# The passage from the adjacency product to the recurrence: the last layer norm in halves on two engines, the recurrence's first step beside it, and VectorE's weight preparation in the last block

## The reference

```python
x = x + relu(adj @ (item_feat @ W_item.T + b_item) + layernorm(x) @ W_user.T + b_user)
u = layernorm(x)
# LSTM over all 10000 tokens, hidden size 128, gates i, f, g, o of W_ih u + W_hh h + b
# g = argmax of two logits of h (0 or 1); w = g * h; inc = cumsum(w)
x = x + 2 * h + (inc - w) * fw_att + (inc[-1] - inc) * bw_att
```

## Time and profile before

| | |
|---|---|
| median of 3 runs | 1463.78 us (1462.88 to 1464.43) |
| the profiled execution | 1465.26 us, of which 1463.4 us are the span of the profile |
| TensorE busy | 1424.2 us (97%) |
| VectorE busy | 1222.9 us (84%) |
| ScalarE busy | 1093.6 us (75%) |
| GpSimd busy | 213.6 us (15%) |
| one block of the product, in the middle | 55.6 us |
| one step of the recurrence | 3.2 us |
| end of the last product of block 19 | 1150.2 us |
| second step of group 0 begins | 1169.5 us |

### The profile page before, as it was taken

One profiled execution on the slowest core, in us unless ns is written; L12 is line 12 of the kernel. 1 busy time (PEld: TensorE's weight loads), 2 busy tenths in 40 slices (PEclk: granted clock), 3 DMA queues, 4 the chain that ended last, 5 costly groups with the idle time before them and its releaser, 6 DMA issues.

```text
span 1463.4 us, 26490 instructions
## 1 busy us (share of the span) xinstructions
PE 1424.2 (97%) x7544; PEld 1224.6 (84%) x7544; DVE 1222.9 (84%) x2050; ACT 1093.6 (75%) x1601; POOL 213.6 (15%) x193
## 2 busy tenths in 40 slices
PE   7999999999999999999999999999999799999994
PEld 6878888888888888888888888888888699999994
DVE  6998889889898898888888888888888566676667
ACT  5668878878878887887887887887887476556662
POOL 0001001001001001001001000000100132027775
PEclk9999999999999999999999999999999899999997
DMA  9889999999999999999999999999999103000003
GB/s 377 317 280 350 394 366 355 389 366 356 384 368 363 378 368 372 375 361 376 362 371 383 366 361 383 362 362 393 358 360 387 71 0 140 0 2 0 1 0 141
DMA packets 129396, 427.99 MB, mean 292 GB/s; under 512 B 15763, under 2 KB 30420, under 8 KB 129238
## 3 DMA queue, kind: packets, MB, share of 16 engines
q1 hardware_dynamic: 127776, 426.43, 77.4%
q10 hardware_dynamic: 1590, 1.18, 0.2%
HBM read 417.30 MB, written 10.24 MB: 292 GB/s over the span
## 4 chain that ended last, share of the span: by engine, by line
issue 77%; PE 15%; POOL 2%; DVE 2%; DMA 2%; ACT 0%; POOLq 0%; SPq 0%; DVEq 0%
PE psZ L872 8%; PE psZ L858 2%; PE psZ L860 2%; PE psZ L862 2%; DMA u<-in_itemT 2%; POOL own L498 1%; PE psZ L878 1%; POOL own L501 1%; DVE u L1278 1%; DVE a_lo L1024 0%; PE psZ L938 0%; POOL run L493 0%; POOL rstd L429 0%; PE psZ L845 0%; POOL u L481 0%
## 5 line engine op out<-in xcount | busy, mean ns | idle before, releaser
L601 ACT ACTIVATE a_hi<-raw 128x1000 fp32r<-128x1000 f32 (+1 forms) x800 | 812.8, 1032 | 228.6 <-PE psG L777 222.5
L1024 DVE TENSOR_TENSOR a_lo<-raw,a_hi 128x1000 fp32r<-128x1000 f32 (+1 forms) x800 | 907.9, 1170 | 72.5 <-ACT a_hi L601 58.4
L775 PE MATMUL psG<-a_hi,item_hi 128*128 128x500 f32 x1560 | 621.3, 398 | 3.5 <-DVE a_lo L1024 3.5
L776 PE MATMUL psG<-a_lo,item_hi 128*128 128x500 f32 x1560 | 606.3, 389 | 0.0
L777 PE MATMUL psG<-a_hi,item_lo 128*128 128x500 f32 x1560 | 604.6, 388 | 0.0
L775 PEld LDWEIGHTS psG<-a_hi,item_hi 128*128 128x128 f32 x1560 | 293.8, 188 | 64.7 <-issue 5.1
L777 PEld LDWEIGHTS psG<-a_hi,item_lo 128*128 128x128 f32 x1560 | 293.4, 188 | 59.4
L776 PEld LDWEIGHTS psG<-a_lo,item_hi 128*128 128x128 f32 x1560 | 294.1, 189 | 58.7 <-issue 4.4
L429 POOL TENSOR_TENSOR rstd<-var,minus_half 125x4 f32<-125x4 f32 x40 | 76.1, 1903 | 1055.8 <-DVE var L1006 1055.8
L872 PE MATMUL psZ<-hist,wh 128*128 (+1 forms) x1264 | 167.0, 275 | 1.2 <-DVE hist L1166 1.1
L872 PEld LDWEIGHTS psZ<-hist,wh 128*128 128x128 f32 x1264 | 154.2, 191 | 1.6 <-issue 1.6
(11 more groups left out here) (151 smaller groups left out, 839.2 us busy)
## 6 DMA issues: line engine op xcount, KB each, us to landing
raw<-in_adj_main SPq DMA_DIRECT2D x760, 500.0 KB, 5.7
raw<-in_adj_main SPq DMA_DIRECT2D x40, 250.0 KB, 3.4
x_copy<-xb SPq DMA_DIRECT2D x20, 250.0 KB, 5.9
u<-x_copy SPq DMA_DIRECT2D x1, 5000.0 KB, 14.6
out<-u SPq DMA_DIRECT2D x25, 200.0 KB, 2.4
xb<-in_xT SPq DMA_DIRECT2D x18, 250.0 KB, 5.3
u<-in_itemT SPq DMA_DIRECT2D x8, 512.0 KB, 11.0
raw<-in_adj_tail SPq DMA_DIRECT2D x60, 31.2 KB, 2.9
```

What stands on the lines that cost most here:

```text
L601: nc.scalar.activation(a_hi[:, s % CUT, 0:n], raw[:, r % RAW, at:at + n], ACT.Copy)\
L775: pe.matmul(bank, w_hi, hi, start=(c == 0), stop=False)
L776: pe.matmul(bank, w_hi, lo, start=False, stop=False)
L1024: last = dve.tensor_tensor(a_lo[:, s % CUT, 0:m], raw[:, r % RAW, at:at + m], a_hi[:, s % CUT, 0:m].bitcast(f32), ALU.subtract)
```

## The change

1. **Weight preparation.** The 12 instructions behind block 0 go into VectorE's last block (`prepare`), at the pieces that table `PREP` names (8, 10, 11, 12, 13). Four more that stood in the passage (`dfb`, `dfd`, `thr`, `wd`) go to pieces 12 and 14 of it.
2. **Step 0 of group 0 early.** Group 0's tokens are complete before the last block, so its step 0 starts right behind the last block's product: TensorE makes 3 products (the forget gate of step 0 meets a zero cell and is dropped) and the 4 products of step 1's input, 125 columns each; ScalarE and VectorE do the gates, cell and state between the pieces of the norm. GpSimd copies the special slots before the last inverse root. The PSUM tiles of the block part change places so that `psG`, `psT` and `psV` don't lie under the gate banks 0 to 3.
3. **The norm in halves.** Relu, addition, transposes and moments run in two halves of 250 tokens; the inverse root is still one. Then ScalarE scales two sub-blocks and VectorE two, TensorE transposes VectorE's two first, each engine writes its own half of `u`, first the slots of steps 0 and 1 (`end_u01`), then the rest.
4. **Opening of the recurrence.** Step 0 and input of step 1 for group 1 follow when `end_u01` says so; then `from_state` of step 1 for both groups with nothing between, and the 12 input products of step 2 behind them, first those without `u_lo`.

The diff, cut to its core:

```diff
@@ PSUM tiles @@
+        psI = pb("psI", [P, 2, 512], first)
+        psW = pb("psW", [P, 512], first)
+        pb("unused_bank", [P, 512], first)
         psG = pb("psG", [P, 2, 512], first)
         psT = pb("psT", [P, SUB * HID], first)
         psV = pb("psV", [P, 512], first)
-        psI = pb("psI", [P, 2, 512], first)
-        psW = pb("psW", [P, 512], first)
@@ GpSimd @@
-            with nc.gpsimd.Fori(1, 2 * NB) as m:
+            with nc.gpsimd.Fori(1, 2 * NB - 1) as m:
                 inv_std(m)
-            pool.wait_ge(u_ready, NB)
+            pool.wait_ge(u_ready, 1)
             pool.tensor_copy(by_step(0, HL, 0, 1), by_step(HL, L, 1, 2)).then_inc(special, 1)
             pool.tensor_copy(by_step(HL, L, 0, 1), by_step(0, HL, 2, 3)).then_inc(special, 1)
+            inv_std(2 * NB - 1)
+            pool.wait_ge(end_u_v, 1)
@@ ScalarE @@
-            relu(NB - 1)
-            normalise(2 * NB - 1)
-            out_u(2 * NB - 1, 1, NB // 2 - 1)
+            act.wait_ge(halves_done, HALVES * NB)
+            for h in range(2):
+                nc.scalar.activation(rl[:, h * HB:(h + 1) * HB], psG[:, 1, h * HB:(h + 1) * HB], ACT.Relu,
+                                     bias=bu[:, 0:1]).then_inc(end_relu, 1)
...
+            first_gates(0)
+            first_cell_tanh(0)
+            act.wait_ge(ln_scale, 2 * NB)
+            for s in range(2):
+                nc.scalar.activation(normed[0:SW, s * HID:(s + 1) * HID], psT[0:SW, s * HID:(s + 1) * HID],
+                                     ACT.Identity, bias=shift_rows[:, s:s + 1], scale=rstd[:, s:s + 1])\
+                    .then_inc(end_normed_a, 1)
+            act.wait_ge(end_back[0], 1)
...
+            nc.scalar.activation(slots[:, K - 11:K - 5, 0:2], whole[:, :, 0:2], ACT.Copy, bias=1.0).then_inc(end_u01, 1)
+            nc.scalar.activation(slots[:, K - 11:K - 6, 2:L], whole[:, 0:5, 2:L], ACT.Copy, bias=1.0)
...
+            act.wait_ge(end_u_v, 1)
+            first_gates(1)
+            first_cell_tanh(1)
...
-            act.wait_ge(pads, 2)
-            for r in range(4):
+            input_hi(1)
+            for r in range(1, 4):
                 lstm(r, r % 2, lambda: input_hi(r + 1))
@@ TensorE @@
-            pe.wait_ge(x1_ready, NB)
-            to_rows(2 * NB - 1, 1)
-            to_columns(2 * NB - 1, u_ready, NB - 1)
+            pe.wait_ge(prep, 17)
+            pe.wait_ge(u_ready, NB - 1)
+            pe.wait_ge(special, 2)
+            from_input_f32(0, 0, 0)
+            from_input_f32(1, 0, 1)
+            for h, rows in enumerate((psT, psV)):
+                pe.wait_ge(end_x1, h + 1)
...
+                for s in range(2):
+                    at = h * HB + s * SW
+                    last = pe.transpose(rows[0:SW, s * HID:(s + 1) * HID], xb[:, 1, at:at + SW], ident[:, :])
+                last.then_inc(end_rows, 1)
...
-            pe.wait_ge(prep, 17)
-            pe.wait_ge(u_ready, NB)
-            pe.wait_ge(special, 2)
-            from_input_f32(0, 0)
-            from_input_f32(1, 1)
-            for n in range(1, 4):
+            pe.wait_ge(end_u01, 2)
+            pe.wait_ge(t1_ready[0], 1)
+            from_input_f32(0, 1, 0)
+            from_input_f32(1, 1, 1)
+            from_state(1, 0, 0, 1)
+            from_state(1, 1, 0, 1)
+            pe.wait_ge(pads, 2)
+            pe.wait_ge(t1_ready[1], 1)
+            pe.wait_ge(hi2_ready, 1)
+            from_input(HI_ONLY, 2, 0)
+            pe.wait_ge(lo2_ready, 1)
+            from_input(LO_ONLY, 2, 0)
+            for n in range(2, 4):
@@ VectorE @@
+            def prepare(r):
+                if r == PREP["wx"]:
+                    dve.wait_ge(wx_psum, 1)
+                    for q0, q1, by in ((0, 2, 0.5), (2, 3, 1.0), (3, 4, 0.5)):
+                        dve.tensor_scalar(wx[:, q0 * HID:q1 * HID], psW[:, q0 * HID:q1 * HID], by, None, ALU.mult)\
+                            .then_inc(prep, 1)
...
             def body(j, has2=True, has1=True, items=False):
                 for r in range(PIECES):
+                    if not has1:
+                        prepare(r)
                     split_lo(j, r, 0)
```

More of the change, by code:

```diff
@@ L47 @@
 SW = BW // SUB
+HB = BW // 2
 QUADS = (CH + 1 + 3) // 4
@@ L67 @@
 PASSES = [(q, part) for q in range(4) for part in range(3)]
+HI_ONLY = [(q, part) for part in (0, 2) for q in range(4)]
+LO_ONLY = [(q, 1) for q in range(4)]
 BETWEEN = 4
@@ L649, in gate_pair @@
                 if bank == 0:
-                    if not (isinstance(n, int) and n == 0 and g == 1):
-                        act.wait_ge(z0_ready[g], n + 1 - g)
+                    act.wait_ge(z0_ready[g], n + 1)
                     nc.scalar.activation(tb(g, 0, 2).rearrange("p (q k) -> p q k", k=KG), zb(g, 0, par), ACT.Tanh)\
@@ L654, in gate_pair @@
                 else:
-                    if not (isinstance(n, int) and n == 0 and g == 1):
-                        act.wait_ge(z1_ready[g], n + 1 - g)
+                    act.wait_ge(z1_ready[g], n + 1)
                     nc.scalar.activation(go[:, g, :].rearrange("p (q k) -> p q k", k=KG), zb(g, 1, par), ACT.Tanh)\
@@ L1128, in _, with first_cell @@
             body(NB - 1, has1=False)
-            add_relu(NB - 1)
-            stats(2 * NB - 1)
+            for h in range(2):
+                dve.wait_ge(end_relu, h + 1)
+                dve.tensor_tensor(xb[:, 1, h * HB:(h + 1) * HB], xb[:, 1, h * HB:(h + 1) * HB],
+                                  rl[:, h * HB:(h + 1) * HB], ALU.add).then_inc(end_x1, 1)
+            for h, rows in enumerate((psT, psV)):
+                dve.wait_ge(end_rows, h + 1)
+                for s in range(2):
+                    dve.bn_stats(moments[:, 2 * h + s, :], rows[0:SW, s * HID:(s + 1) * HID]).then_inc(ln_moments, 1)
             pair_up(2 * NB - 1)
             eps(2 * NB - 1)
-            row_scale(2 * NB - 1)
-            dve.wait_ge(u_ready, NB)
+            def first_cell(g):
+                dve.wait_ge(t1_ready[g], 1)
+                dve.scalar_tensor_tensor(group(C, g), tb(g, 0), 1.0, go[:, g, 0:KG], ALU.add, ALU.mult)\
+                    .then_inc(c_ready[g], 1)
+            first_cell(0)
+            dve.wait_ge(halves_done, HALVES * NB)
             for t in (u_hi, u_lo):
@@ L1139, in _ @@
                                   ALU.mult).then_inc(pads, 1)
-            dve.memset(C[:, :], 0.0).then_inc(zeroed, 1)
-            dve.wait_ge(prep, 15)
-            dve.tensor_tensor(dfb[:, :], hfw[:, :], mbw[:, :], ALU.add).then_inc(dfb_ready, 1)
-            dve.wait_ge(dfb_ready, 1)
-            dve.tensor_scalar(dfd[:, :], ident[:, :], dfb[:, 0:1], None, ALU.mult).then_inc(dfd_ready, 1)
-            dve.tensor_scalar(thr[:, :], thr0[:, :], 2.0, None, ALU.mult).then_inc(wd_ready, 1)
-            dve.tensor_scalar(wd[:, :], ones[:, :], wdc[:, 0:1], None, ALU.mult).then_inc(wd_ready, 1)
-            dve.wait_ge(zeroed, 1)
+            row_scale(2 * NB - 1)
+            dve.wait_ge(ln_scale, 2 * NB)
+            for s in range(2, SUB):
+                dve.tensor_scalar(normed[0:SW, s * HID:(s + 1) * HID], psV[0:SW, (s - 2) * HID:(s - 1) * HID],
+                                  rstd[:, s:s + 1], shift_rows[:, s:s + 1], ALU.mult, ALU.add)\
+                    .then_inc(end_normed_v, 1)
+            slots = steps_view()
             def forget_product(n, g):
@@ L1192, in lstm_pair @@
                 lstm(W + 2 * i + 3, 2 * i + 3)
-            with nc.vector.Fori(0, W // 4) as i:
+            state(0, 0, 0)
+            dve.wait_ge(end_back[1], 1)
+            whole = psG[:, 1, HB - 6 * L:HB].rearrange("p (s l) -> p s l", l=L)
+            dve.tensor_scalar(slots[:, K - 5:K + 1, 0:2], whole[:, :, 0:2], 1.0, None, ALU.add).then_inc(end_u01, 1)
+            dve.tensor_scalar(slots[:, K - 5:K + 1, 2:L], whole[:, :, 2:L], 1.0, None, ALU.add)
+            dve.tensor_scalar(slots[:, K - 6:K - 5, L - (HB - 6 * L):L], psG[:, 1, 0:HB - 6 * L].unsqueeze(1), 1.0,
+                              None, ALU.add).then_inc(end_u_v, 1)
+            first_cell(1)
+            state(0, 1, 0)
+            for r in range(1, 4):
+                lstm(r, r)
+            with nc.vector.Fori(1, W // 4) as i:
                 for r in range(4):
```

102 lines of the change are left out of this document (75 added, 27 removed).

## The result

| | before | after |
|---|---|---|
| median, in the comparison that was predicted | 1463.99 us (1462.88 to 1464.43, 4 runs) | 1454.6 us (1453.81 to 1456.39, 4 runs) |
| profiled execution | 1465.26 us | 1454.52 us |
| span of the profile | 1463.4 us | 1452.7 us |

The ratio is 0.9936, 95% interval 0.9924 to 0.9949: faster by 9.4 us. Forecast: 1453.7, range 1451.2 to 1456.6.

A forecast was written before the change was run, and what follows sets the result against it. TensorE, busy 97%, was taken as the bound, so gains come from less waiting or full clock. Terms 4.45 + 0 + 5.6 = 10.05 us off the 1463.78 median gave 1453.7 us, range 1451.2 to 1456.6.

The forecast's parts named there:

- Part 1: End of block 0: without the weight preparation TensorE's stall and its low clock go; gain 4.45 us, bounds 0 to 4.51.
- Part 2: Last block: the preparation moved there hides in VectorE's slack; cost 0, bounds 0 and 0.5 us.
- The 0.24 us of room at piece 8: Last block, tightest place: a_lo done at 1118.0, TensorE starting that half at 1118.24.
- Part 3: Passage from the blocks' last product to step 2 of group 0: starts 5.6 us earlier, bounds 4.4 to 6.5.
- the 0.35: Norm in the passage: moments start after two of four transposes, so halving gains 0.35 us.
- The +0.2: Last inverse root in the passage: 1.01 us grows by 0.2 beside VectorE's work, possible range 0 to +0.9.
- the forecast's 3.9: Passage: full clock returns 3.9 us after group 1's input products begin at 1157.12.
- 0.3 us to spare: Passage: ScalarE's and VectorE's work for steps 0 and 1 fits beside TensorE's products with 0.3 us left.
- Nothing in block 1: Rival at block 1: loads may set the pace once the stall is gone, so no gain there; 1458.2 us, chance 0.08.
- Half the passage: Rival in the passage: late hand-overs and clock 2 us later lose some 3 us; 1456.8 us, chance 0.07.
- The low clock stays: Rival after the passage: steady steps cost 6.44 us instead of 3.22; eight give 1479.5 us, chance 0.04.
- Never low: Rival in the passage: TensorE keeps full clock, group 1's gates path bounds step 2 at 1162.05; 1451.9 us, chance 0.07.

The follow-up runs named there:

- e6_whole_relu: The changed kernel with the last relu and the addition each in one piece of 500 tokens instead of halves; 1455.62 us, a single run, passage 14.86 us.
- e1_prep_only: The kernel before with only the 12 weight-preparation instructions moved from behind block 0 to the last block; 1459.97 us beside 1464.13, ratio 0.9971.
- the first experiment: The kernel before with only the 12 weight-preparation instructions moved to the last block; 1459.97 us, ratio 0.9971, block 0's last product to block 1's 55.78 us.
- by the second: The changed kernel with the 12 weight-preparation instructions put back behind block 0; 1459.92 us, ratio 0.9965, passage 14.34 us.
- the filled wait: The changed kernel with step 1's four input products behind the transposes to rows, done three times; 1452.61 us, ratio 0.9923; again 1451.57 us, ratio 0.9916.
- four behind: The changed kernel with step 1's four input products moved behind the transposes to rows; 1454.78 us, ratio 0.994; again 1454.09 us, ratio 0.9927.

## Why the prediction was right

**Part 1, forecast 4.45.** Measured 4.32 in the profile and 4.16 between the medians of the kernel that does it alone. The step's mechanism stood as worked out: the wait goes, the clock stays at 1.00, nothing takes the stall's place. Block 1 takes 55.79 where block 2 takes 55.60. Of these 0.19 us, 0.07 are the start of its first product, 0.30 us behind the last instead of 0.23, for which the forecast had left 0.06; the rest, about the 0.13 missing, no run takes apart.

**Part 2, forecast 0.** The last block takes 54.73 us against 54.74, and 54.72 in the kernel that changes nothing else. The 0.24 us of room at piece 8 were enough.

**Part 3, forecast 5.6.** Measured 5.03 in the first execution of the changed kernel, 6.20 (19.69 - 13.49) in the second and 5.35 (19.69 - 14.34) in the kernel that has only the passage; the mean is 5.5, and the two medians of the changed kernel, 1454.6 and 1453.14, lie on either side of the forecast's 1453.7. That the forecast comes this near to the mean is in part luck, as terms that were off cancel. By its terms:
- The transposes start 1.79 us after the last product begins; forecast 1.78. The moments end at 3.11 us (1147.28); forecast 3.13. So the 0.35 for starting them after two of the four transposes came, though no run takes it away alone. What was wrong is that the halves of relu and addition gain nothing: `e6_whole_relu` shows 0.31 us for them.
- The inverse root takes 1.01 us. The +0.2 allowed for its neighbours isn't there, although VectorE works on the cell and the padding beside it. The rule cited from the Trainium skill (GPSIMD Engine Reference, Key points) names instructions with two SBUF inputs or in a two-port mode. Neither the cell (one operand in PSUM) nor the padding (one input) has two SBUF inputs, and whether the padding runs in a two-port mode no trace shows; the 1.01 us show no contention with either. Beside `a_lo`, which has two, the same operation still takes 1.90, as the rule has it.
- VectorE's two sub-blocks take 0.73, not 0.5, which uses up what the inverse root left over: the transposes back start at 5.81 us, forecast 5.78. That is luck.
- Group 1's products begin at 7.20; the forecast's 1157.12 is 7.30 in that count. At the low clock a product takes 0.449 (3.14 us from 1151.37 to 1154.51, for seven); 0.46 was taken.
- The clock returns 4.8 us after these products begin, not 3.9. That is the term that was mis-sized: 0.9 us longer at half speed is 0.45 of the 0.57 us missing. In the second execution it is 3.0 and the passage 0.6 shorter than forecast; with the passage alone it is 4.1. A single number could not be right here; the forecast's 3.9 lies among those that occur.
- The gates and cells nearly fitted beside it. The forecast had 0.3 us to spare, but inside group 1's state products the weight load waits 0.20 us for ScalarE's tanh (at 1156.85), and the products lose about as much (an estimate: at the two prices above they would be done at 1157.14, and step 2's input starts at 1157.32). This is the other part of what is missing.

**Where the 5.03 us come from.** The early step gives 1.66, the split 0.60 and the halves of relu and addition 0.20 (by the passages of the kernels without each, one profile apiece, so each is uncertain by the 0.3 us found above). The other 2.6 us were not taken apart by a run. By the timeline they are the copy to `u` and GpSimd's slots, which no longer stand ahead of the products (0.28 us of waiting where 1.85 were), the moments that start sooner, and a low clock of 6.83 us instead of 10.24. What the clock cost before is less than it looks. In `e1_prep_only`, whose passage is that of the kernel before, the low clock stood 1 us later and the fp32 products ended 0.5 us later, and step 2 still began at 19.69: in the kernel before the input of step 2 waits for GpSimd's `u_lo`, and in that experiment it starts at the same 17.3 us without a wait. The row of the kernel before, then that of the experiment:

```profile
1167.09 0.39 PE L858 MATMUL psZ<-u_hi,wx_hi 128*128 128x256 f32 x1 [0.27 <-POOL u_lo L451]
```

```profile
1162.02 0.38 PE L858 MATMUL psZ<-u_hi,wx_hi 128*128 128x256 f32 x1
```

So what the shorter low clock gave can't simply be counted on top of the rest.

**The rivals.** *Nothing in block 1* is refuted by the first experiment. *Half the passage* by the second (14.34 us; the rival's 3 us more than forecast mean 17.1). *The low clock stays* didn't happen in the passage of any profile: the longest stretch was 10.24 us, and from step 2 to the end it is 293.87 us against 293.89. *Never low* didn't happen in the changed kernel, but the filled wait shows that it was priced well: step 2 at 11.99 us, where the rival's 1162.05 means 12.23, and a time of 1452.6 and 1451.6 against 1451.9. With it ScalarE's path did become the next bound, the rounding of step 2's input included, as that rival said; its wait, though, was 0.29 us for group 0's tanh and not for group 1's gates.

## What to carry to other kernels

A wait of a few microseconds of TensorE costs twice, once as idle time and again as slow products behind it. So price a passage with the clock as a term of its own, with a range instead of a value, and look at more than one execution before crediting an order of instructions with a microsecond. Where the wait itself can't be removed, work repeated into it can be worth more than a better order: here against the same order without the filling it took 1.2 and 2.4 us from the passage, 2.2 and 2.5 from the median (the first pair on two chips, the second on one), and most of the spread between runs (1.1 and 0.8 us where 3.7 and 3.5 were). Small, independent preparation belongs where the engine has slack on every turn of a loop, not between two blocks that hand over tightly.

## What the runs showed of the hardware

- With 3.4 us of idle time and some 1.3 us of short transposes behind it, the granted clock was 0.50 for 6.83 us in one execution of a program and for 3.41 in another; with 2.4 us idle it was 3.42 and 6.83. With 4.6 us idle (the kernel before) it was 10.24; with 0.6 us it stayed at 1.00 throughout the passage. 3.4 us more at the low clock made this passage 1.2 us longer (11.99 to 13.23, 13.23 to 14.43, 13.49 to 14.66), not the 1.7 of half speed alone; part of the time it falls on TensorE's waits (0.6 us of the one ahead of the transposes back, in the first execution of the changed kernel).
- An fp32 product of 125 columns takes 0.222 us at the full clock and 0.449 at the low one.
- GpSimd's inverse root of 125x4 takes 1.01 us beside VectorE's work on a cell and a padding tile, and 1.90 beside its subtraction of two 128x1000 tiles.
- The beginning of block 0's last product moves by up to 2.7 us over the thirteen profiles, and by up to 1.7 between two executions of one kernel (88.03 and 89.69 with four behind). No run told what it comes from.
